# Layer one of a two-layer graph network: per-group statistics by one 128x512 product, sums and statistics added by two operations a tile

## The chip, the cores and the metric

One NeuronCore of one Trainium2 chip runs the whole program. The metric is the device time of one execution in microseconds. Engines are named as in the profile: PE is TensorE (PEld its weight loads), DVE is VectorE, ACT is ScalarE, POOL is GpSimd, SP is SyncE.

## What is computed

Two graph layers over 6,250 nodes of 128 channels and 106,250 edges sorted by destination. Only layer one is changed:

```python
h = jnp.maximum(_layernorm(x, axis=-1), 0.0)
x = nodes @ W + b_lin                      # nodes = h; 4 heads of 32 channels
sent, recvd = x[snd], x[rcv]
logits = leaky_relu(sum(concat(sent, recvd) * alpha, -1), 0.2)
e = jnp.exp(logits - segment_max(logits, rcv)[rcv])
att = e / segment_sum(e, rcv)[rcv]
out = segment_sum(att[:, :, None] * sent, rcv) + bias
```

The kernel needs, for every destination node, the weighted sum of its senders' rows (128 channels) and five statistics: two sums of weights, a count, and two maxima. A product with a 0/1 mask (edge x node) makes both from the edges of a tile.

## The kernel before

**Tiles, groups, rounds.** The edges are padded to 832 tiles of 128 edges. Four tiles (`TG`) are a group (208 groups), eight groups (`RG`) a round; the first and last round have four groups (`SPANS`). Below, k = 0 to 7 is a group's place in its round.

**POOL (L472).** One indirect DMA per tile gathers 128 rows of 130 numbers into a ring of 24 groups (`RING`). Before group g POOL waits until PE has finished group g - 24 (`agg0`).

**PE (L948 to L974).** For group g, `sum_stats` waits until DVE has added group g - 2 (`acc0`), then makes four products, one a tile: 5 columns of `edge_w` as weights, the tile's 128x128 mask moving, out to 5 lines of `stat_sums` at lines 32t, columns 128t. `sum_group` then makes four full products with the gathered rows as weights into `row_sums` and signals `agg0`. Sums and statistics of a group lie in two neighbouring banks of PSUM (`both_sums`), two such pairs in turn. At k = 0 `spread_delta` puts four one-column products (L937, L939) between the two.

**DVE (L663 to L691).** For group g it waits for `agg0`, then for each of the four tiles it makes the mask of a tile two groups on (L665) and adds sums and statistics of the tile in one operation of 128 lines by 2x128 numbers (L670) into `acc2`, at a column that a register gives. Each add first waits for the add before it (`acc0`), because their destinations overlap. Scaling of rows by their weights (L679) stands before a group, penalties (L603 to L615) after k = 0.

**Between rounds.** After k = 7, DVE scans the next round's logits for segment maxima (L625 to L651), with small PE transposes in between (L917 to L947). ACT makes the weights (L1138) and writes them into `edge_w` (L1144). Only then can k = 0 of the next round go through PE.

**End of layer one.** The last six groups' masks (`EARLY`) are made one round ahead. From L796 on, while the last two rounds run, finished blocks of nodes are transposed (L989, L995), divided and added to x. No gathers run from about 1343 us to 1476 us.

Of the kernel before, what the change touches and what calls it, by code (L numbers as in the profile page):

```python
# [7 lines left out]
P = 128  # L8
# [6 lines left out]
SH = 2  # L15
NB = (N + P - 1) // P
NPAD = NB * P
UA = 3
# [4 lines left out]
TG = 4  # L23
GE = TG * P
# [3 lines left out]
TILES = GROUPS * TG  # L28
ROUNDS = GROUPS // RG
EPAD = TILES * P  # L30
RT = RG * TG
# [3 lines left out]
LCOL = 5  # L35
RW = CH + SH
FW = CH + HEADS
Q4 = P // TG
# [8 lines left out]
WORK = UNITS_A + RAW // UA  # L47
# [5 lines left out]
RG1 = 12  # L53
WORK1 = UNITS + RAW1
PROJ_SLOTS = 3
LINE_SLOTS = 3
ACT_BATCH = 16
ACT_TURNS = 2
ACT_ROUND = P // ACT_TURNS
# [15 lines left out]
EARLY = range(GROUPS - 6, GROUPS)  # L75
# [11 lines left out]
def gnn_layers(nc, a, out, table1, table2, table3):  # L87
# [3 lines left out]
    ds = bass.ds  # L91

    ctx = ExitStack()
    with ctx:
# [3 lines left out]
        def sb(name, shape, dt=fp32, st=ctx):  # L98
            return st.enter_context(nc.sbuf_tensor(name, shape, dt))
# [23 lines left out]
        def sem(name):  # L123
            return ctx.enter_context(nc.semaphore(name))
# [4 lines left out]
        both_sums = [pair[n][:, :, :] for n in range(2)]  # L129
        row_sums = [bank[0], bank[2]]  # L130
        stat_sums = [bank[1], bank[3]]
# [5 lines left out]
        acc2 = sb("acc2", [P, 2, ACCW])  # L137
        acc = acc2[:, 0, :]
        acc_w = acc2[:, 1, :]
# [9 lines left out]
        onehot = sb("onehot", [P, 2, TG, P])  # L149
# [9 lines left out]
        with ExitStack() as st:  # L159
# [6 lines left out]
            own_scale, sum_scale = parts[:, 1], parts[:, 0]  # L166
            rows_x = sb("rows_x", [P, LINE_SLOTS, RW], st=st)
            offsets = sb("offsets", [FETCHED, P], i32, st)
            bias_all = sb("bias_all", [P, CH], st=st)
            dst_pair = sb("dst_pair", [P, 2 * TILES], i32, st)  # L170
            dst_int, first_all = dst_pair[:, 0:TILES], dst_pair[:, TILES:]
            IN_PAIR = 2 * TILES // P
            early_a = dst_pair[:, 0:IN_PAIR * P].bitcast(fp32).rearrange("p (t c) -> p t c", c=P)
            early_b = sb("early_b", [P, len(EARLY) * TG - IN_PAIR, P], st=st)
            dn = sb("dn", [SH * (RT + 2) - 2, 2, P + 2], i32, st)
# [18 lines left out]
            select_w = sb("select_w", [1, SH, P], st=st)  # L194
            factor = sb("factor", [P, 1], st=st)
            factor_w = sb("factor_w", [P, 1], st=st)
            edge_w = sb("edge_w", [P, 2, RT, LCOL], st=st)
            sizes = sorted({z for _, z in SPANS})
            pens = {z: sb(f"pens{z}", [1, 2, SH * (z * TG + 2)], st=st) for z in sizes}
            edge_of = {z: sb(f"edge_of{z}", [1, 2, SH * (z * TG + 2)], st=st) for z in sizes}  # L200
# [2 lines left out]

            normed = sb("normed", [P, 2, UA, CH], st=st)
            feats_t = sb("feats_t", [P, 2, UA * P], st=st)
            moments0 = sb("moments0", [P, WORK * UA, 6], st=st)
            mean_var0 = sb("mean_var0", [P, WORK * UA, 2], st=st)
            rows_w = moments0[:, :, :].rearrange("p m s -> p (m s)")[:, 0:2 * RW].rearrange("p (k c) -> p k c", k=2)
            std0 = sb("std0", [P, WORK * UA], st=st)
            rstd0 = sb("rstd0", [P, WORK * UA], st=st)  # L210
            shift0 = sb("shift0", [P, WORK * UA], st=st)
            w0 = sb("w0", [P, CH], st=st)
            w0_t = sb("w0_t", [P, CH], st=st)
            w0_ext = sb("w0_ext", [P, FW], st=st)
# [47 lines left out]
            def converted(r):  # L262
# [4 lines left out]
            bias_in, biased, dn_used, set_done, sc = (  # L267
                sem(n) for n in ("bias_in", "biased", "dn_used", "set_done", "sc"))
# [6 lines left out]
            oh0, scaled0, scaled_v, agg0, acc0 = (sem(n) for n in ("oh0", "scaled0", "scaled_v", "agg0", "acc0"))  # L275
            half_in = [sem(f"half_in{s}") for s in range(RING // HALF)]
            line_in = [sem(f"line_in{s}") for s in range(LINE_SLOTS)]
            lines_in, offsets_ready = sem("lines_in"), sem("offsets_ready")
# [73 lines left out]
            def line_total(j):  # L352

                return 16 * P * (j // LINE_SLOTS + 1)

            def row_of(n):

                if n in LINE_TILES:
                    return rows_x[:, LINE_TILES.index(n) % LINE_SLOTS, :]
                if n in ACT_TILES0:  # L360
# [9 lines left out]
            def mask_of(n):  # L370

                i = n - EARLY.start * TG
                if i < 0:
                    return onehot[:, n // TG % 2, n % TG, :]
                return early_a[:, i, :] if i < IN_PAIR else early_b[:, i - IN_PAIR, :]

            def scale_parts(g):

                n, end = g * TG, (g + 1) * TG
                cuts = sorted({n, end, *(x + d for x in LINE_TILES + ACT_TILES0 for d in (0, 1) if n <= x + d < end)})  # L380
                return list(zip(cuts, cuts[1:]))

            def scaled_until(g):

                return sum(len(scale_parts(v)) for v in range(g + 1))
# [18 lines left out]
            def first_sync(sp):  # L404
# [9 lines left out]
                def line(j):  # L414
                    if j >= LINE_SLOTS:
                        sp.wait_ge(agg0, LINE_TILES[j - LINE_SLOTS] // TG + 1)
                    for o in range(0, P, BATCH):
# [107 lines left out]
            def first_vector(dve):  # L525
# [1 line left out]
                dve.memset(stat_sums[1][:, :], 0.0).then_inc(set_done, 1)  # L527
                dve.memset(select[:, :, :], 0.0).then_inc(set_done, 1)
                dve.memset(select_w[:, :, :], 0.0).then_inc(set_done, 1)
                dve.memset(edge_w[:, :, :, SH:SH + 1], 1.0).then_inc(set_done, 1)  # L530
                for z in sizes:
                    dve.memset(pens[z][:, :, :], -BIG).then_inc(set_done, 1)
                    dve.memset(edge_of[z][:, :, :], -BIG).then_inc(set_done, 1)
                    dve.memset(lg_cols[z][:, :], 0.0).then_inc(set_done, 1)
                dve.wait_ge(set_done, 5 + 3 * len(sizes))
                for h in range(SH):
                    dve.memset(select[:, h, h * HC:(h + 1) * HC], 1.0).then_inc(set_done, 1)
                    dve.memset(select_w[:, h, h::Q4], 1.0).then_inc(set_done, 1)
# [46 lines left out]
                dve.wait_ge(dst_in, 16 * 2)  # L585
                dve.tensor_tensor(dst_rel[:, :], dst_int[:, :], first_all[:, :], ALU.subtract).then_inc(rel_done, 1)
                dve.wait_ge(bias_in, 16)
                dve.wait_ge(set_done, 5 + 2 * SH + 3 * len(sizes))
                dve.wait_ge(rel_done, 1)
                done = [0]  # L590

# [73 lines left out]
                    dve.tensor_scalar(mask_of(n), iota_row[:, :], dst_rel[:, n:n + 1], None, ALU.is_equal).then_inc(early_ready if n // TG in EARLY else oh0, 1)  # L665

                def add(n, v):
                    if n:
                        dve.wait_ge(acc0, n)
                    dve.tensor_tensor(acc2[:, :, ds(v, P)], acc2[:, :, ds(v, P)], both_sums[n // TG % 2][:, :, n % TG * P:(n % TG + 1) * P],  # L670
                                      ALU.add).then_inc(acc0, 1)

                def scale_rows(r, g):

# [150 lines left out]
                n = (g1 + 2) * TG  # L825
# [9 lines left out]
                n = (g1 + 3) * TG  # L835
# [25 lines left out]
            def first_tensor(pe):  # L861
# [40 lines left out]
                    last.then_inc(own_t, 1)  # L902
                for w in range(UNITS_A):
                    turn_own(w)
                pe.wait_ge(set_done, 5 + 2 * SH + 3 * len(sizes))

                def turn_penalties(r):
                    n, step = lines(r), SH * pitch(r)
# [40 lines left out]
                def sum_stats(r, g):  # L949
                    k = g - SPANS[r][0]  # L950
                    if k == 0:
                        pe.wait_ge(ew_ready, 2 * (r + 1))
                    if g in EARLY:
                        pe.wait_ge(early_ready, (g + 1 - EARLY.start) * TG)
                    else:
                        pe.wait_ge(oh0, (g + 1) * TG)
                    if g >= 2:
                        pe.wait_ge(acc0, (g - 1) * TG)
                    for t in range(TG):
                        pe.matmul(stat_sums[g % 2][t * Q4:t * Q4 + LCOL, t * P:(t + 1) * P], edge_w[:, r % 2, k * TG + t, :], mask_of(g * TG + t),  # L960
                                  start=True, stop=True)
                    if k == 0:
                        spread_delta(r)

# [81 lines left out]
            def first_scalar(act):  # L1046
# [52 lines left out]
                    act.copy(acc[SH * HC:, starts(w) * P:starts(w) * P + m], row_sums[w % 2][SH * HC:, 0:m]).then_inc(own_in, 1)  # L1099
                for w in range(UNITS_A):  # L1100
                    keep_own(w)
                act.wait_ge(set_done, 5 + 2 * SH + 3 * len(sizes))

                def keep_logits(r):
                    if r < RAW_TURNS:
# [619 lines left out]
```

## Time and profile before

| | us |
|---|---|
| median of 3 runs | 2840.2 (2838.53 to 2845.22) |
| profiled execution, its own time | 2840.72 |
| its span, first to last instruction | 2838.9 |
| PE / DVE / ACT / POOL busy | 1705.1 / 1536.6 / 588.7 / 1601.2 |
| L472, gathers of layer one, x782 | 742.7 busy, 950 ns each |
| L973, group sums, x1616 records | 382.3 busy, 411 ns each |
| L960, statistics, x1616 records | 116.3 busy, 377 ns each |
| L670, add of sums and statistics, x832 | 349.5 busy, 420 ns each |
| L665, masks in the loop, x808 | 235.6 busy, 292 ns each |

A timeline row gives start, busy time, engine, line, operation, out<-in, how many instructions were merged (x), and in brackets the idle time of the engine before it with what ended it. An fp32 product shows as two records, so x8 stands for four tiles. "remote" means that the profile did not find who released the wait. PEclk is the granted TensorE clock as a share of 2.4 GHz.

### The profile page before, as it was taken

The page shows a single profiled execution, that of the slowest core. Times are in us where ns is not written, and L with a number is a line of the kernel's source. Part 1 is how long each engine was busy: PE and PEld are TensorE (multiplying, and loading weights), DVE is VectorE, ACT ScalarE, POOL GpSimd, SP SyncE. Part 2 cuts the span into 40 slices and gives each one's busy share as a digit, 9 for nine tenths or more (in the row PEclk, how much of TensorE's full clock was granted, in tenths as well). Part 3 has the DMA queues.
Part 4 walks back from the last instruction along what each step waited for, and adds up shares of the span by engine and source line. Part 5 has one row for each costly group of instructions (what it writes and reads, how often), then busy time and mean ns, then how long its engine had stood idle before and what let it go on. Part 6 is the DMA issues. An engine that isn't in the chain of part 4 may idle for free.

```text
span 2838.9 us, 30406 instructions
## 1 busy us (share of the span) xinstructions
PE 1705.1 (60%) x8785; PEld 1185.5 (42%) x8785; DVE 1536.6 (54%) x5409; ACT 588.7 (21%) x1218; POOL 1601.2 (56%) x1703
## 2 busy tenths in 40 slices
PE   1444545444444444444644877787787787777778
PEld 1333334233333333333434544554454554454556
DVE  1455556554555545556754555555555555555557
ACT  1530000000000000000235333333333233333333
POOL 6425666665566665656063566666666665566650
PEclk6765555555555555555667888887888778888889
DMA  4201221221122111211042333333333333344332
GB/s 122 71 21 40 46 45 44 46 45 43 39 46 46 43 44 42 46 42 45 1 114 71 105 106 95 106 109 110 109 110 111 111 96 100 107 110 112 109 105 79
DMA packets 102330, 212.33 MB, mean 75 GB/s; under 512 B 30944, under 2 KB 65238, under 8 KB 92183
## 3 DMA queue, kind: packets, MB, share of 16 engines
q0 software_dynamic: 53120, 109.70, 15.7%
q1 hardware_dynamic: 46411, 99.73, 12.3%
q8 instruction: 72, 1.18, 0.2%
q10 hardware_dynamic: 2636, 0.98, 0.2%
q14 instruction: 91, 0.75, 0.1%
HBM read 197.40 MB, written 12.88 MB: 74 GB/s over the span
## 4 chain that ended last, share of the span: by engine, by line
PE 31%; DVE 23%; another core or an unknown queue 21%; issue 19%; ACT 4%; DVEq 1%; POOL 0%; DMA 0%; ACTq 0%; SPq 0%; POOLq 0%
DVE acc L670 9%; PE pair L1424 6%; PE bank L1433 6%; PE bank L1444 5%; PE pair L1418 4%; PE pair L973 4%; DVE onehot L665 2%; DVE acc L1627 2%; DVE onehot L1586 2%; DVE pre L1612 1%; PE pair L960 1%; DVE ef L1593 1%; PE bank L937 1%; ACT hidden L1503 1%
## 5 line engine op out<-in xcount | busy, mean ns | idle before, releaser
L1367 POOL DMA_INDIRECT acc<-table,index x830 | 786.1, 947 | 533.6 <-DVE pre L1612 268.5
L472 POOL DMA_INDIRECT rows<-table,index x782 | 742.7, 950 | 539.8 <-issue 214.5
L1627 DVE TENSOR_TENSOR acc<-acc,bank 128x128 f32 x832 | 239.5, 288 | 411.6 <-remote 188.0
L665 DVE TENSOR_SCALAR onehot<-iota_row,dst_rel 128x128 f32<-128x128 f32 x808 | 235.6, 292 | 408.3 <-remote 326.3
L1424 PE MATMUL pair<-hidden,we 128*128 128x512 f32 x416 | 281.6, 764 | 210.6 <-ACT hidden L1503 152.3
L973 PE MATMUL pair<-onehot,rows 128*128 128x128 f32 x1616 | 382.3, 411 | 0.0
L973 PEld LDWEIGHTS pair<-onehot,rows 128*128 128x128 f32 x1616 | 328.0, 301 | 68.6 <-issue 61.1
L1433 PEld LDWEIGHTS bank<-wn1b,ef 128*128 128x128 f32 x1664 | 273.3, 237 | 193.4 <-issue 100.6
L670 DVE TENSOR_TENSOR acc<-acc,pair 128x256 f32 x832 | 349.5, 420 | 5.4 <-PE pair L973 1.8
L1433 PE MATMUL bank<-wn1b,ef 128*128 128x128 f32 x1664 | 280.6, 324 | 52.4 <-DVE ef L1593 44.1
L1444 PE MATMUL bank<-onehot,msg 128*128 128x128 f32 x1664 | 261.9, 309 | 13.4 <-ACT msg L1516 8.8
L960 PE MATMUL pair<-onehot,edge_w 128*5 128x128 f32 x1616 | 116.3, 377 | 247.2 <-DVE acc L670 214.9
L1444 PEld LDWEIGHTS bank<-onehot,msg 128*128 128x128 f32 x1664 | 243.2, 225 | 18.9 <-ACT msg L1516 14.2
L1418 PE MATMUL pair<-ea,we 64*128 64x512 f32 x416 | 248.2, 678 | 0.0
L1503 ACT ACTIVATE hidden<-pair,be 128x512 f32<-128x512 f32 x208 | 141.2, 679 | 431.8 <-remote 293.5
L1424 PEld LDWEIGHTS pair<-hidden,we 128*128 128x128 f32 x416 | 71.2, 215 | 382.1 <-issue 192.6
L1516 ACT ACTIVATE msg<-pre 128x512 f32<-128x512 f32 x208 | 131.0, 630 | 426.7 <-DVE pre L1612 356.9
L1138 ACT ACTIVATE weights<-shifted 66x128 f32<-66x128 f32 (+1 forms) x27 | 8.3, 309 | 994.2 <-DVE shifted L650 835.5
L1593 DVE SCALAR_TENSOR_TENSOR ef<-pair,be,gate 128x512 f32<-128x512 f32 x208 | 155.4, 747 | 95.2 <-remote 51.0
L923 PE MATMUL bank<-ident,seg_max 66*1 66x66 f32 (+1 forms) x54 | 10.0, 287 | 308.9 <-issue 193.8
L1586 DVE TENSOR_SCALAR onehot<-iota_row,dst_rel 128x128 f32<-128x128 f32 x832 | 186.5, 291 | 0.1
L1612 DVE TENSOR_TENSOR pre<-bank,acc 128x512 f32<-128x512 f32 x208 | 142.4, 685 | 62.8 <-remote 37.9
(170 smaller groups left out, 1466.6 us busy)
## 6 DMA issues: line engine op xcount, KB each, us to landing
ts<-in_ts SPq DMA_DIRECT2D x52, 1024.0 KB
ea<-in_ea_t SPq DMA_DIRECT2D x52, 512.0 KB
acc<-table,index POOLq DMA_INDIRECT x830
rows<-table,index POOLq DMA_INDIRECT x782
table<-feat SPq DMA_DIRECT2D x16, 195.0 KB
table<-proj SPq DMA_DIRECT2D x12, 256.0 KB, 2.3
table<-x_rows SPq DMA_DIRECT2D x11, 256.0 KB, 2.3
out<-x_rows SPq DMA_DIRECT2D x11, 256.0 KB
```

Source lines behind the costliest of these rows:

```text
L472: gp.indirect_dma_start(rows0[:, n % (RING * TG), :], None, table1, bass.IndirectOffsetOnAxis(index[:, n:n + 1], 0)).then_inc(half_in[g % ...
L665: dve.tensor_scalar(mask_of(n), iota_row[:, :], dst_rel[:, n:n + 1], None, ALU.is_equal).then_inc(early_ready if n // TG in EARLY else oh0, 1)
L670: dve.tensor_tensor(acc2[:, :, ds(v, P)], acc2[:, :, ds(v, P)], both_sums[n // TG % 2][:, :, n % TG * P:(n % TG + 1) * P], ALU.add).then_i ...
L973: last = pe.matmul(row_sums[g % 2][:, t * P:(t + 1) * P], row_of(g * TG + t)[:, 0:CH], mask_of(g * TG + t), start=True, stop=True)
L1367: gp.indirect_dma_start(rows[:, g % RG1, t, :], None, table, bass.IndirectOffsetOnAxis(index[:, n:n + 1], 0)).then_inc(gathered[g % RG1], 16)
L1418: pe.matmul(bank[g % 2][:, :], we1[:, :], ea[:, g // HALF % 2, edges(g)], start=True, stop=True).then_inc(h1, 1)
L1424: pe.matmul(bank[2 + g % 2][:, :], we2[:, :], hidden[:, g % 2], start=True, stop=True).then_inc(h2, 1)
L1433: last = pe.matmul(bank[4 + g % 2][:, t * P:(t + 1) * P], ef[:, g % 2, t * P:(t + 1) * P], wn1b[:, :], start=True, stop=True)
L1444: last = pe.matmul(bank[6 + g % 2][:, t * P:(t + 1) * P], msg[:, g % 2, t, :], onehot[:, g % 2, t, :], start=True, stop=True)
L1586: dve.tensor_scalar(onehot[:, g % 2, t, :], iota_row[:, :], dst_rel[:, q:q + 1], None, ALU.is_equal).then_inc(oh1, 1)
L1593: dve.scalar_tensor_tensor(ef[:, g % 2], bank[2 + g % 2][:, :], be2[:, 0:1], gate[:, g % 2], ALU.add, ALU.mult).then_inc(efd, 1)
L1627: dve.tensor_tensor(acc[:, ds(v, P)], acc[:, ds(v, P)], bank[6 + g % 2][:, t * P:(t + 1) * P], ALU.add).then_inc(acc1, 1)
```

## The change

Each group's four statistics products become one: 32 columns (`Q4`) of `edge_w` per tile, five used and the rest zero, 4x32 = 128 weight columns, against the four masks side by side (128x512), a full bank of `stat_sums`. Tile t's statistics are the block of lines 32t and columns 128t, as before; the twelve mixed blocks are not read. The add becomes two operations: 32 lines by 128 of the statistics into `acc_w` with no wait of its own, then 128 by 128 of the sums into `acc` behind the `acc0` wait. `edge_w` grows and is cleared once at the start. To make room and to let a group's masks lie side by side, `early_a`/`early_b` are cut at whole groups, the opening layer norm's small buffers share the place of `early_b`, and an unused buffer shrinks.

```diff
-LINE_SLOTS = 3
+LINE_SLOTS = 1
...
-            IN_PAIR = 2 * TILES // P
+            IN_PAIR = 2 * TILES // GE * TG
...
-            edge_w = sb("edge_w", [P, 2, RT, LCOL], st=st)
+            edge_w = sb("edge_w", [P, 2, RT, Q4], st=st)
...
+            opening = early_b[:, :, :].rearrange("p t c -> p (t c)")
+            NS = WORK * UA
+            moments0 = opening[:, 0:6 * NS].rearrange("p (m s) -> p m s", s=6)
+            mean_var0 = opening[:, 6 * NS:8 * NS].rearrange("p (m s) -> p m s", s=2)
...
+            def masks_at(g):
+
+                i = (g - EARLY.start) * TG
+                if i < 0:
+                    return onehot[:, g % 2, :, :]
+                return early_a[:, i:i + TG, :] if i < IN_PAIR else early_b[:, i - IN_PAIR:i - IN_PAIR + TG, :]
...
-                dve.memset(edge_w[:, :, :, SH:SH + 1], 1.0).then_inc(set_done, 1)
+                dve.memset(edge_w[:, :, :, :], 0.0).then_inc(set_done, 1)
...
+                dve.memset(edge_w[:, :, :, SH:SH + 1], 1.0).then_inc(set_done, 1)
...
                 def add(n, v):
+                    b, t = n // TG % 2, n % TG
+                    own_lines, own_cols = slice(t * Q4, (t + 1) * Q4), slice(t * P, (t + 1) * P)
+                    dve.tensor_tensor(acc_w[own_lines, ds(v, P)], acc_w[own_lines, ds(v, P)], stat_sums[b][own_lines, own_cols], ALU.add)
                     if n:
                         dve.wait_ge(acc0, n)
-                    dve.tensor_tensor(acc2[:, :, ds(v, P)], acc2[:, :, ds(v, P)], both_sums[n // TG % 2][:, :, n % TG * P:(n % TG + 1) * P],
-                                      ALU.add).then_inc(acc0, 1)
+                    dve.tensor_tensor(acc[:, ds(v, P)], acc[:, ds(v, P)], row_sums[b][:, own_cols], ALU.add).then_inc(acc0, 1)
...
-                    for t in range(TG):
-                        pe.matmul(stat_sums[g % 2][t * Q4:t * Q4 + LCOL, t * P:(t + 1) * P], edge_w[:, r % 2, k * TG + t, :], mask_of(g * TG + t),
-                                  start=True, stop=True)
+                    pe.matmul(stat_sums[g % 2], edge_w[:, r % 2, k * TG:(k + 1) * TG, :].rearrange("p t c -> p (t c)"),
+                              masks_at(g).rearrange("p t c -> p (t c)"), start=True, stop=True)
```

## Rows read from the trace of the kernel before

**Rows 1.** Windows: us, busy (count) of PE, PEld, DVE, ACT, POOL, PEclk, DMA, GB/s

```profile
197.00:1343.00 1146.00, 530.48 (x3409) 392.56 (x3407) 622.45 (x2300) 30.07 (x151) 695.54 (x732) 0.56 0.20 44
1343.00:1476.00 133.00, 77.27 (x534) 58.80 (x535) 100.84 (x347) 36.85 (x142) 37.27 (x46) 0.65 0.17 46
```

**Rows 2.** Timeline of ACT: the weights of a round, once a round

```profile
225.75 0.31 ACT L1138 ACTIVATE weights<-shifted 66x128 f32<-66x128 f32 x1 [20.30 <-DVE shifted L650]
...
669.67 0.31 ACT L1138 ACTIVATE weights<-shifted 66x128 f32<-66x128 f32 x1 [43.10 <-DVE shifted L650]
...
721.91 0.31 ACT L1138 ACTIVATE weights<-shifted 66x128 f32<-66x128 f32 x1 [43.26 <-DVE shifted L650]
...
1319.70 0.31 ACT L1138 ACTIVATE weights<-shifted 66x128 f32<-66x128 f32 x1 [39.64 <-DVE shifted L650]
```

**Rows 3.** Timeline of POOL: the gathers that follow a wait

```profile
526.22 0.94 POOL L472 DMA_INDIRECT rows<-table,index  x1 [4.29 <-PE pair L973]
...
543.53 0.94 POOL L472 DMA_INDIRECT rows<-table,index  x1 [2.46 <-remote]
...
560.85 0.94 POOL L472 DMA_INDIRECT rows<-table,index  x1 [2.61 <-remote]
...
574.94 0.94 POOL L472 DMA_INDIRECT rows<-table,index  x1 [4.29 <-PE pair L973]
...
761.03 0.94 POOL L472 DMA_INDIRECT rows<-table,index  x1 [1.18 <-remote]
```

**Rows 4.** Timeline of DVE: after k = 0, k = 3, k = 6, and at the scan

```profile
204.27 0.28 DVE L779 TENSOR_TENSOR x_rows<-x_rows,bias_all 128x128 f32<-128x128 f32 x1
204.47 0.22 DVE L603 CAST line<-dn 66x130 f32<-66x130 int32 x1
...
543.29 0.29 DVE L665 TENSOR_SCALAR onehot<-iota_row,dst_rel 128x128 f32<-128x128 f32 x1 [4.35 <-remote]
...
560.61 0.29 DVE L665 TENSOR_SCALAR onehot<-iota_row,dst_rel 128x128 f32<-128x128 f32 x1 [9.08 <-remote]
560.81 0.42 DVE L670 TENSOR_TENSOR acc<-acc,pair 128x256 f32 x1
...
561.14 0.28 DVE L665 TENSOR_SCALAR onehot<-iota_row,dst_rel 128x128 f32<-128x128 f32 x1
...
565.02 0.41 DVE L625 TENSOR_TENSOR_SCAN fore<-pen_f,bank 66x128 f32<-66x128 f32 x1
```

**Rows 5.** Timeline of PE: k = 3, k = 6, then k = 0 of the next round

```profile
533.85 2.08 PE L973 MATMUL pair<-onehot,rows 128*128 128x128 f32 x8
...
548.81 1.62 PE L973 MATMUL pair<-onehot,rows 128*128 128x128 f32 x8
...
570.26 0.61 PE L960 MATMUL pair<-onehot,edge_w 128*5 128x128 f32 x8 [0.48 <-ACT edge_w L1144]
570.80 1.01 PE L937 MATMUL bank<-delta,select 1*128 1x1 f32 x4
...
572.59 2.08 PE L973 MATMUL pair<-onehot,rows 128*128 128x128 f32 x8
```

**Rows 6.** Waits of DVE from 197 to 1343 us: total, times, longest

```profile
DVE onehot L665 <- remote: 326.3, 58, 9.1
```

**Rows 7.** Timeline of PE in layer two: a full product of 128x512

```profile
2004.31 1.12 PE L1418 MATMUL pair<-ea,we 64*128 64x512 f32 x2
...
2014.55 2.08 PE L1424 MATMUL pair<-hidden,we 128*128 128x512 f32 x2 [5.23 <-ACT hidden L1503]
```

**Rows 8.** Windows around k = 0: columns as in rows 1

```profile
570.00:575.00 5.00, 4.74 (x32) 3.79 (x32) 1.91 (x7) 0.44 (x4) 0.71 (x2) 0.50 0.13 28
```

**Rows 9.** Timeline of the stretch without gathers: PE, then DVE without masks

```profile
1348.34 0.61 PE L960 MATMUL pair<-onehot,edge_w 128*5 128x128 f32 x8 [0.50 <-DVE acc L670]
...
1416.33 2.06 DVE L670 TENSOR_TENSOR acc<-acc,pair 128x256 f32 x4
...
1417.01 1.16 PE L973 MATMUL pair<-dst_pair,rows 128*128 128x128 f32 x8
```

More of the change, by code:

```diff
@@ L205, in gnn_layers @@
             feats_t = sb("feats_t", [P, 2, UA * P], st=st)
[L206 to L211, printed above, removed]
+            opening = early_b[:, :, :].rearrange("p t c -> p (t c)")
+            NS = WORK * UA
+            moments0 = opening[:, 0:6 * NS].rearrange("p (m s) -> p m s", s=6)
+            mean_var0 = opening[:, 6 * NS:8 * NS].rearrange("p (m s) -> p m s", s=2)
+            rows_w = opening[:, 0:2 * RW].rearrange("p (k c) -> p k c", k=2)
+            std0, rstd0, shift0 = (opening[:, (8 + i) * NS:(9 + i) * NS] for i in range(3))
             w0 = sb("w0", [P, CH], st=st)
@@ L587, in first_vector @@
                 dve.wait_ge(bias_in, 16)
-                dve.wait_ge(set_done, 5 + 2 * SH + 3 * len(sizes))
+                dve.wait_ge(set_done, 6 + 2 * SH + 3 * len(sizes))
                 dve.wait_ge(rel_done, 1)
@@ L904, in first_tensor @@
                     turn_own(w)
-                pe.wait_ge(set_done, 5 + 2 * SH + 3 * len(sizes))
+                pe.wait_ge(set_done, 6 + 2 * SH + 3 * len(sizes))
                 def turn_penalties(r):
@@ L1101, in first_scalar @@
                     keep_own(w)
-                act.wait_ge(set_done, 5 + 2 * SH + 3 * len(sizes))
+                act.wait_ge(set_done, 6 + 2 * SH + 3 * len(sizes))
                 def keep_logits(r):
```

## Prediction

> **What bounds the kernel now.** I read the windows by stage first. From 197 to 1343 us, layer one's rounds with gathers, no engine is full: of 1146 us PE is busy 530, DVE 622, POOL 696 [rows 1]. So a chain through several engines sets the time. The timeline of ACT shows its beat: L1138 runs once a round, 22 rounds lie between 225.75 and 1319.70, 49.7 us each; single rounds take 48.7 or, as from 669.67 to 721.91, 52.2 [rows 2]. Then I followed one round on POOL, DVE and PE side by side. POOL stands exactly one ring ahead: after 526.22, 543.53, 560.85 and 574.94 it runs on only when a wait has ended [rows 3]. DVE resumes 0.24 us before POOL at 543.29 and 560.61 [rows 4], so both wait for the same signal, `agg0` of k = 3 and of k = 6. The odd thing is that PE had long done both: k = 3 ended at 533.85 + 2.08 = 535.93 and k = 6 at 548.81 + 1.62 = 550.43 [rows 5]. The signals are seen 7.4 and 10.2 us later, both times about 2.5 us after POOL has run out of gathers it may issue [rows 3]. These late signals are DVE's "remote" waits, 326 us in all [rows 6]. Who holds them the profile does not say; it says that they come when POOL stops. Where no gathers run they are absent: there PE waits 0.50 us for DVE's add of two groups before [rows 9].
>
> So a round has three pieces, counted between POOL's restarts: 526.22 to 543.53 (17.3 us) and 543.53 to 560.85 (17.3) are twelve gathers each plus waits, (17.32 - 2.61) / 12 = 1.23 us a gather [rows 3]; 560.85 to 574.94 (14.1) is serial work. In the serial piece DVE adds k = 6 and k = 7 (560.61 to 565.02, eight tiles, 0.55 each) [rows 4], scans, PE turns and ACT makes weights until 570.26, then PE makes the statistics of k = 0 in 0.54 us, the one-column products in 1.79, the sums in 2.08, and POOL restarts [rows 5, 3]. Only this piece is bound by PE's and DVE's own speed.
>
> **Statistics by one product.** Removed: four 5-column products, eight records, from 570.26 to 570.80, 0.54 us [rows 5]. Their records last about 0.38 us each and still eight fit into 0.61, so they overlap. Added: one product of 128x512. Its price is in layer two: 2.08 us at half clock, 1.12 at full clock [rows 7]. At k = 0 the granted clock is 0.50 [rows 8]; PE has then done little for over ten microseconds. I take 2.08: +1.54 us at k = 0 of every round, on the path. At full clock it would be 1.12 against 0.40, about +0.7: that is the lower end. For k = 1 to 7 the same +1.54 lies beside waits: PE's chain for k = 3 grows by at most 4 x 1.54 = 6.2 us less what already waits for DVE, and k = 3's signal has 7.4 us to spare; k = 6's chain, counted from k = 3's signal, passes k = 4 to 6, grows by at most 4.6 and has 10.2. So nothing shows as long as the lateness keeps its date. If that cover is gone, it costs 1.54 a product. What is late next is POOL's wait for k = 2: its run of eight gathers after 526.22 would stop a microsecond or two, inside the piece that ends at 543.53.
>
> Eight records of four products show 0.61 us where a single full-width product of the same 512 columns shows 2.08 [rows 5, 7]. The Trainium skill, page "TensorEngine Tiling (Array Packing)", section "Overview", gives up to four times the speed for a side of at most 32, which this change gives up; rows and rule agree. The same page, section "Key Properties", says that a change of tiling mode drains TensorE. That rule speaks for the change, which removes two mode changes a group. By the rule there would be a gain outside the four products; the rows leave it no more than a share of the 0.54, since 570.80 follows 570.26 by just that.
>
> **Two operations for one add.** Before: mask and add together take 0.55 us a tile; the add of 256 columns lasts 0.42, then the next add waits for it and starts about 0.14 later, and the mask hides in between [rows 4]. After: mask, statistics add, sums add. The trace has no 32x128 add. Slots nearest to it are start to start: mask to next 0.20 (560.61 to 560.81), a 128x128 add to next 0.20 (204.27 to 204.47) [rows 4]. Three slots give 0.60; one more register instruction a tile may show, so I take 0.63, +0.08 a tile. Lower end: 0, if slots pack a little closer; upper end: three full busy times of 0.28, 0.84, +0.29. The wait for the sums add before no longer shows, since two operations lie behind it. On the path are the eight tiles of k = 6 and 7: 8 x 0.08 = +0.6 us a round (0 to 2.3). The adds of k = 0 to 5, +0.3 a group, lie under the same late signals as the products. Where no masks are made (last groups), four adds take 2.06 us [rows 9]; two short operations with an add chain of 0.28 + 0.14 give about 1.7, -0.3 a group.
>
> **Costed at nothing.** Clearing `edge_w` (2048 numbers a line) at the start, a few microseconds at most on DVE: the opening waits for x and the biases, and waits later hide it. The shared buffers, the wider stride of `edge_w` for ACT's writes: same sizes of operations. No DMA or POOL instruction is added or moved.
>
> **The sum.** Rounds with gathers: 22 x (1.54 + 0.64) = 22 x 2.18 = 48.0 us. Outside of them: k = 0 of the first short round +1.5; the round after 1319.70, of which only part has gathers, +3.5; the 16 full groups from 1361 to 1419 without gathers: PE has 0.50 us of slack a group [rows 9], so each costs between 0.3 (DVE sets the pace) and 1.0 (PE does), 0.6 taken, 9.6, and their two k = 0 +3.1; the last four groups +3.0; eight groups without masks -2.4. Together +18.3. Layer two is untouched. 48.0 + 18.3 = +66.3 on the profiled execution's 2840.7 gives 2907.0; that execution lies 0.5 above the median of 2840.2, so I forecast 2907 (rounded). A measurement of this kernel tells 0.3%, 8.5 us, from no change.
>
> **The rivals.** *(a) The lateness is a delay after PE's end, not a date set by POOL.* Then what makes k = 3 and k = 6 end later passes through. At half clock k = 3 ends some 2.9 us later (k = 1 to 3 back to back in PE at 4.1 us each against 9.95 us now) and k = 6 some 3.3: +6.2 a round on top, 22 x 6.2 = 136, 3043 us. At full clock products shrink by as much as the new one adds, and little is left; halfway is 2975. For it: the same lateness of the second signal in most rounds. Against it: each signal falls about 2.5 us behind POOL's stop [rows 3]. Chance 0.2.
>
> *(b) The extra serial time is taken back by shorter stops.* The waits of POOL that end "remote" are 2.61 us at 560.85 but 1.18 at 761.03 [rows 3]. If products that end later make them 1.2 instead of 2.5, two a round give back 2.6 of the 2.2: about 2845 with the tail. Chance 0.12.
>
> *(c) Faster: the clock.* PE does more in the same time; if that keeps the granted clock at 1.0 up to k = 0, the serial piece has 1.12 for the product, 1.79 / 2 = 0.9 for the one-column products and 1.16 for the sums [rows 7, 9], 3.2 instead of 4.4, with DVE's +0.6 a gain of 0.6 a round: 22 x 0.6 = 13 us, tail about even, 2828. It decides from the point where the clock at k = 0 is over 0.75. Against it: PE idles through the scan whatever the product takes, and rows 8 show 0.50. Chance 0.08; other gains 0.02.
>
> *(d) Other beat.* Rounds of 48.7 and of 52.2 us exist [rows 2], six of the 22 are long. All long would be 16 x 3.5 = +56 on my sum, 2963; none long -21, 2886. This widens my case, it isn't one of its own.
>
> **How the numbers follow.** My case, with 2870 to 2965 as its own range, has 0.5; (a) 0.2; (b) 0.12; (c) and other gains 0.1; what I have not thought of on the slow side 0.08. Predicted is the likeliest, 2907. The range for 8 in 10 leaves out (c) and the upper part of (a): 2846 to 2990. Faster by over 0.3%: 0.10; within: 0.12; slower: 0.78.
>
> **What would show it.** In the profile of the changed kernel: L960 as two records, about 2.08 us together, with the one-column products 2.1 instead of 0.54 us behind its start; the way from DVE's start on k = 6 to POOL's restart 16.3 us instead of 14.1; tiles at 0.63 us; POOL's pieces of twelve gathers still near 17.3; L1138 about 51.9 us apart. A piece of twelve gathers of 19 us or more means (a); a beat still under 50 means (b); a PEclk of 1.0 at k = 0 means (c). I would be wrong above all if the unknown holder of PE's signals depends on PE's instructions themselves, since the change takes six product records and six weight loads a group out of PE's stream.

## The result and the profile after

The changed kernel takes 2944.8 us (median of 4 runs, 2941.4 to 2951.7), the kernel before 2842.7 beside it: ratio 1.036, 95% interval 1.034 to 1.039. It is slower by 102 us; forecast was 2907, +66. The kernel before itself took 2837 to 2867 us in some of the later comparisons and 2168 to 2176 us in others (one slow execution of 2523 us left out), one and the same chip among both, so that every kernel is set against the runs of before made beside it, and those of the first kind are called "beside 2843", those of the second "beside 2172".

The timeline of ACT of the changed kernel, the line that makes a round's weights (L1147, before L1138) [rows 2], shows where the time went:

```profile
228.18 0.31 ACT L1147 ACTIVATE weights<-shifted 66x128 f32<-66x128 f32 x1 [19.95 <-DVE shifted L658]
282.65 0.31 ACT L1147 ACTIVATE weights<-shifted 66x128 f32<-66x128 f32 x1 [42.77 <-DVE shifted L658]
...
609.54 0.31 ACT L1147 ACTIVATE weights<-shifted 66x128 f32<-66x128 f32 x1 [43.08 <-DVE shifted L658]
661.51 0.31 ACT L1147 ACTIVATE weights<-shifted 66x128 f32<-66x128 f32 x1 [40.60 <-issue]
...
1402.66 0.31 ACT L1147 ACTIVATE weights<-shifted 66x128 f32<-66x128 f32 x1 [43.17 <-DVE shifted L658]
...
1520.22 0.31 ACT L1147 ACTIVATE weights<-shifted 34x128 f32<-34x128 f32 x1 [12.74 <-DVE shifted L658]
```

The same 22 rounds take 1174.5 us (228.18 to 1402.66) instead of 1093.9: +80.5. Up to the first of them +2.4. From the last to the last weights of all 117.6 us instead of 99.7 (1319.70 to 1419.37): +17.9. From there to the end of the span 1419.4 instead of 1419.5: layer two pays nothing. Together +100.7, the difference of the two spans, 2939.6 and 2838.9. There are again two kinds of rounds: 52.0 us (609.54 to 661.51; nine of them, 51.9 on average) and 54.4 (228.18 to 282.65; thirteen), where before had sixteen of 48.8 and six of 52.2 on average [rows 2].

The timeline of POOL, those gathers that follow a stop, says what sets the two kinds. A run is here the gathers between two stops, and a piece is a run with the stop that ends it:

```profile
562.65 0.94 POOL L479 DMA_INDIRECT rows<-table,index  x1 [9.55 <-PE pair L982]
...
579.90 0.94 POOL L479 DMA_INDIRECT rows<-table,index  x1 [2.30 <-PE pair L982]
...
602.75 0.94 POOL L479 DMA_INDIRECT rows<-table,index  x1 [3.10 <-remote]
...
617.00 0.94 POOL L479 DMA_INDIRECT rows<-table,index  x1 [9.55 <-PE pair L982]
...
634.23 0.94 POOL L479 DMA_INDIRECT rows<-table,index  x1 [2.33 <-PE pair L982]
...
651.50 0.94 POOL L479 DMA_INDIRECT rows<-table,index  x1 [2.60 <-remote]
...
668.97 0.94 POOL L479 DMA_INDIRECT rows<-table,index  x1 [7.79 <-PE pair L982]
```

From 617.00 to 668.97 POOL runs twelve gathers, twelve and eight, each followed by a stop: 17.23, 17.27 and 17.47 us. Before, the same three pieces took 17.31, 17.32 and 14.09 [rows 3]. The first two are as they were; all of +3.38 lies in the serial piece. From 562.65 to 617.00 the runs are twelve, sixteen and four, and the piece that ends with k = 0 takes 14.25 though it holds four gathers only: k = 6 was added before it, k = 7 in it (DVE starts on them at 594.73 and 602.52). Other long rounds have twelve, twelve, four and four, like the long ones of before.

The serial piece itself, on DVE (k = 6 from 651.27, its scan at 657.59) and on PE:

```profile
651.27 0.29 DVE L673 TENSOR_SCALAR onehot<-iota_row,dst_rel 128x128 f32<-128x128 f32 x1 [6.68 <-remote]
651.47 0.27 DVE L678 TENSOR_TENSOR acc<-acc,pair 32x128 f32 x1
651.66 0.27 DVE L681 TENSOR_TENSOR acc<-acc,pair 128x128 f32 x1
651.86 0.27 DVE L673 TENSOR_SCALAR onehot<-iota_row,dst_rel 128x128 f32<-128x128 f32 x1
652.16 0.28 DVE L678 TENSOR_TENSOR acc<-acc,pair 32x128 f32 x1
652.46 0.29 DVE L681 TENSOR_TENSOR acc<-acc,pair 128x128 f32 x1
...
657.59 0.41 DVE L633 TENSOR_TENSOR_SCAN fore<-pen_f,bank 66x128 f32<-66x128 f32 x1
```

```profile
662.82 2.08 PE L969 MATMUL pair<-onehot,edge_w 128*128 128x512 f32 x2 [0.47 <-ACT edge_w L1153]
664.83 1.01 PE L947 MATMUL bank<-delta,select 1*128 1x1 f32 x4
665.71 0.99 PE L949 MATMUL bank<-delta,select_w 1*128 1x1 f32 x4
666.62 2.08 PE L982 MATMUL pair<-onehot,rows 128*128 128x128 f32 x8
```

The eight tiles take 6.32 us (651.27 to 657.59), before 4.41 (560.61 to 565.02) [rows 4]: +1.91, 0.24 a tile. The product takes 2.01 us until the next begins (662.82 to 664.83), before 0.54 [rows 5]: +1.47. The two make the whole 3.38. The slots show where the tile loses: its first three operations start 0.20 us apart, but in the second tile, whose statistics are on lines 32 to 63, L678 starts 0.30 after the mask and L681 0.30 after L678, each just behind the end of the operation in front (651.86 + 0.27, 652.16 + 0.28). Six of the eight tiles have two such slots. The third tile of each group has a longer mask as well (0.34 and 0.48 us, at 652.66 and 655.75), and the add behind it waits for that too; why this mask is longer no run tells.

The windows, and the waits of DVE, of the changed kernel (columns as in rows 1 and 6):

```profile
197.00:1343.00 1146.00, 563.43 (x2132) 379.91 (x2132) 709.54 (x2822) 27.36 (x138) 650.65 (x684) 0.70 0.19 41
662.80:668.70 5.90, 5.88 (x19) 4.36 (x20) 1.54 (x5) 0.23 (x2) 0.00 (x0) 0.50 0.00 0
```

```profile
DVE onehot L673 <- remote: 170.5, 41, 6.7
```

In the same stretch the mean granted clock is 0.70 instead of 0.56 [rows 1], yet around k = 0 it is still 0.50, the lower level, 1.2 GHz, and the product takes 2.08 us. DVE's wait for late signals is 170.5 us instead of 326.3 [rows 6]: DVE is busy for 87 us more in it, and the longer adds seem to fill part of the time in which it had waited.

### The profile page after: what moved, and what is told of

Same layout as the page of the kernel before. It is cut to its first block, busy times and chain, and to the rows that moved or that the text cites. A ratio compares the mean times of both kernels' runs of the same rounds, so it can differ in the third digit from the quotient of the medians.

```text
span 2939.6 us, 29540 instructions
## 1 busy us (share of the span) xinstructions
PE 1804.9 (61%) x7537; PEld 1211.5 (41%) x7537; DVE 1693.0 (58%) x6242; ACT 588.4 (20%) x1218; POOL 1603.3 (55%) x1703
## 4 chain that ended last, share of the span: by engine, by line
PE 29%; DVE 28%; issue 21%; another core or an unknown queue 16%; ACT 4%; DVEq 2%; POOL 0%; ACTq 0%; POOLq 0%
DVE acc L681 7%; DVE acc L678 6%; PE pair L1433 6%; PE bank L1442 5%; PE bank L1453 5%; PE pair L1427 4%; PE pair L982 3%; PE pair L969 3%; DVE acc L1636 3%; DVE onehot L673 3%; DVE onehot L1595 2%; DVE pre L1621 1%; DVE ef L1602 1%; PE bank L947 1%
## 5 line engine op out<-in xcount | busy, mean ns | idle before, releaser
L969 PE MATMUL pair<-onehot,edge_w 128*128 128x512 f32 x404 | 316.5, 876 | 258.6 <-DVE acc L681 163.9
L673 DVE TENSOR_SCALAR onehot<-iota_row,dst_rel 128x128 f32<-128x128 f32 x808 | 237.0, 294 | 256.8 <-remote 173.7
L982 PEld LDWEIGHTS pair<-onehot,rows 128*128 128x128 f32 x1616 | 295.5, 259 | 128.4 <-issue 117.7
L982 PE MATMUL pair<-onehot,rows 128*128 128x128 f32 x1616 | 297.0, 345 | 0.0
L678 DVE TENSOR_TENSOR acc<-acc,pair 32x128 f32 x832 | 235.1, 283 | 40.6 <-issue 20.8
L1427 PE MATMUL pair<-ea,we 64*128 64x512 f32 x416 | 255.3, 696 | 0.0
L681 DVE TENSOR_TENSOR acc<-acc,pair 128x128 f32 x832 | 236.2, 284 | 30.8 <-issue 22.5
L1147 ACT ACTIVATE weights<-shifted 66x128 f32<-66x128 f32 (+1 forms) x27 | 8.4, 309 | 1035.2 <-DVE shifted L658 710.1
L969 PEld LDWEIGHTS pair<-onehot,edge_w 128*128 128x128 f32 x404 | 83.0, 255 | 283.7 <-DVE onehot L673 142.9
```

The lines of the kernel that those rows point to most:

```text
L678: dve.tensor_tensor(acc_w[own_lines, ds(v, P)], acc_w[own_lines, ds(v, P)], stat_sums[b][own_lines, own_cols], ALU.add)
L681: dve.tensor_tensor(acc[:, ds(v, P)], acc[:, ds(v, P)], row_sums[b][:, own_cols], ALU.add).then_inc(acc0, 1)
L969: pe.matmul(stat_sums[g % 2], edge_w[:, r % 2, k * TG:(k + 1) * TG, :].rearrange("p t c -> p (t c)"), masks_at(g).rearrange("p t c -> p (t ...
L982: last = pe.matmul(row_sums[g % 2][:, t * P:(t + 1) * P], row_of(g * TG + t)[:, 0:CH], mask_of(g * TG + t), start=True, stop=True)
L1427: pe.matmul(bank[g % 2][:, :], we1[:, :], ea[:, g // HALF % 2, edges(g)], start=True, stop=True).then_inc(h1, 1)
```

## The experiments

**Theories.** *Serial:* only what lies between DVE's start on k = 6 and the sums of k = 0 costs time, 1.47 for the product and 1.8 to 1.9 for the adds; the rest is hidden under the late signals. *Delay:* what the products add at k = 1 to 7 passes through as well. For the adds: *held* (an operation on other lines than the last waits for its end) against *third operation* (it costs as such).

**One half of the change at a time, beside 2843.** product_only keeps before's add (and has the change's buffers):

```
-for t in range(TG):
-    pe.matmul(stat_sums[g % 2][t * Q4:t * Q4 + LCOL, t * P:(t + 1) * P], edge_w[:, r % 2, k * TG + t, :], mask_of(g * TG + t), ...)
+pe.matmul(stat_sums[g % 2], edge_w[:, r % 2, k * TG:(k + 1) * TG, :]..., masks_at(g)..., start=True, stop=True)
 dve.tensor_tensor(acc2[:, :, ds(v, P)], acc2[:, :, ds(v, P)], both_sums[...], ALU.add).then_inc(acc0, 1)
```

> The kernel before with the change's single product of 128 by 512 a group, and the one add of 256 columns kept; what the product puts into the mixed blocks is added too, so the statistics are not the reference's. If the new product costs its own time at k = 0 alone (1.47 us in the trace of the change, L969 at 610.85 to L947 at 612.86 against 0.54): 22 x 1.47 = 32 us in the rounds, 1.5 in the first short round, some 3 in the round after the last full beat, some 10 to 14 in the stretch without gathers: +48 us, 2891, and ACT's weights 51.2 us apart on average. If what products delay at k = 1 to 7 passes through as well, each piece of twelve gathers grows from 17.3 to over 19 us and the time is 2940 or more. If the later product is taken back by shorter stops: under 2860.

adds_only keeps before's four products:

```
-dve.tensor_tensor(acc2[:, :, ds(v, P)], acc2[:, :, ds(v, P)], both_sums[...], ALU.add).then_inc(acc0, 1)
+dve.tensor_tensor(acc_w[own_lines, ds(v, P)], acc_w[own_lines, ds(v, P)], stat_sums[b][own_lines, own_cols], ALU.add)
+dve.tensor_tensor(acc[:, ds(v, P)], acc[:, ds(v, P)], row_sums[b][:, own_cols], ALU.add).then_inc(acc0, 1)
```

> The kernel before with the change's two adds a tile, and the four small products kept. If a tile of 0.775 us instead of 0.55 is on the path for the eight tiles of k = 6 and k = 7 alone: 22 x 1.8 = 40 us, and some 10 to 15 in the stretch without gathers: +53 us, 2896. The sum of this run's and product_only's difference should then be the whole change's +102 within 10 us. If the slower tile comes only together with the wide product (a wait for PE rather than DVE's own pace): no more than +20, 2863.

Measured: product_only 2899.2, ratio 1.020 (1.016 to 1.024); adds_only 2911.3, ratio 1.025 (1.021 to 1.029). The ratios add up to +4.5%, the change shows +3.6%. Both halves cost time, each 8 to 15 us more than expected, and their sum, +124 us, lies 22 above the change's +102 where 10 was the most expected: they are not additive. ACT's weights split the two profiled runs: product_only +48.7 in the 22 rounds and +2.2 in the stretch behind them; adds_only +51.4 and +12.9. POOL's stops in product_only show what its rounds are made of:

```profile
336.77 0.95 POOL L479 DMA_INDIRECT rows<-table,index  x1 [4.92 <-PE pair L980]
...
353.27 0.95 POOL L479 DMA_INDIRECT rows<-table,index  x1 [1.64 <-issue]
...
365.33 0.95 POOL L479 DMA_INDIRECT rows<-table,index  x1 [2.36 <-remote]
...
663.01 0.94 POOL L479 DMA_INDIRECT rows<-table,index  x1 [2.99 <-remote]
...
692.23 0.94 POOL L479 DMA_INDIRECT rows<-table,index  x1 [9.44 <-PE pair L980]
...
715.00 0.94 POOL L479 DMA_INDIRECT rows<-table,index  x1 [2.99 <-remote]
```

Some of its early rounds run twelve, eight and twelve gathers with stops of 1.6, 2.4 and 4.9 us, 48.2 to 48.4 us a round, less than before's short ones in spite of the product. From 530 us on all run sixteen and sixteen with stops of 3.0 and 7 to 11 us, 48 to 56 us. The 32 gathers take some 39.5 us in either; the round is these and its stops, and where the stops fall decides more than 1.47 us do. *Delay* in its full size falls: all rounds would have been some 6 us dearer, and the pieces of twelve outside the serial one are here 16.5 us (336.77 to 353.27), not over 19. But the 22 rounds cost 2.2 us each on average, not 1.47, and what brings the sixteens about, the products of k = 1 to 7 perhaps, no run tells. adds_only runs twelve, eight, twelve in nearly every round, with other stops:

```profile
568.17 0.94 POOL L472 DMA_INDIRECT rows<-table,index  x1 [2.60 <-remote]
...
590.87 0.94 POOL L472 DMA_INDIRECT rows<-table,index  x1 [8.03 <-PE pair L975]
...
602.51 0.94 POOL L472 DMA_INDIRECT rows<-table,index  x1 [1.75 <-PE pair L975]
...
619.81 0.94 POOL L472 DMA_INDIRECT rows<-table,index  x1 [2.61 <-remote]
```

22.70, 11.64 and 17.30, together 51.6.

The same kernel once more, on another chip, where before took 2851.7:

> The kernel before with the change's two adds a tile and its own four small products at every k, the same kernel as adds_only. Where before takes some 2172 us: k0_small differs from it only in the single products of k = 1 to 7. If these lie hidden beside DVE's adds: k0_small_b's 2209 within 4 us, ratio 1.017, the weights of a round 39.1 us apart. If they count: 7 x 1.5 = 10 us a round less, which POOL's 40 us of gathers then cut off, 2185 to 2195. Where before takes some 2840 us: 2911 again.

2972.4, ratio 1.044 (1.038 to 1.049): the same runs of gathers, but the long stop is 9.5 us in nearly all rounds, against 7.4 to 9.5 in adds_only's, and a round takes 53.6 instead of 52.1. So the adds alone cost between 2.5% and 4.4% from one chip to another; a run of it beside 2172, which would separate the adds from the products of k = 1 to 7, is missing.

**Why a tile is slow.** Two kernels, alike but for the lines; the two lines with own_lines are in q0_scratch alone, own_scratch keeps the change's. The statistics are left out of both outputs:

```
+scratch = feats_t[:, :, :].rearrange("p k c -> p (k c)")
-own_lines = slice(t * Q4, (t + 1) * Q4)
+own_lines = slice(0, Q4)
-dve.tensor_tensor(acc_w[own_lines, ds(v, P)], acc_w[own_lines, ds(v, P)], stat_sums[b][own_lines, own_cols], ALU.add)
+dve.tensor_tensor(scratch[own_lines, own_cols], acc_w[own_lines, ds(v, P)], stat_sums[b][own_lines, own_cols], ALU.add)
```

> The changed kernel, but the statistics add of every tile reads and writes lines 0 to 31, and its result goes to a spare place, so the statistics are left out of the output. Same number and sizes of operations as own_scratch. If the tile's 0.775 us come from operations that start on lines other than the last one's and are held until it has finished, all three slots are 0.20 and a tile is 0.60 to 0.63: 1.4 us less a round for eight tiles, 22 x 1.4 = 31 us, and up to 8 in the stretch without gathers: 30 to 39 us under own_scratch. If the cost is that of a third operation as such: no difference to own_scratch (within 3 us).

> The control of q0_scratch: the statistics add goes to the same spare place but on the lines that the change gives it (0, 32, 64, 96 for the four tiles); the statistics are left out of the output. Expected at the changed kernel's time, 2945, within 5 us, with tiles of 0.775 us, if the place of the result costs nothing; 5 to 10 less if the computed address of the output cost time.

Measured: 2939.7 and 2940.3, where *held* had forecast 30 to 39 us between them. By the times alone it would have fallen; the traces say otherwise. The second tile of a group in own_scratch has the held slots of the change:

```profile
600.62 0.27 DVE L673 TENSOR_SCALAR onehot<-iota_row,dst_rel 128x128 f32<-128x128 f32 x1
600.91 0.28 DVE L680 TENSOR_TENSOR feats_t<-acc,pair 32x128 f32<-32x128 f32 x1
601.21 0.29 DVE L683 TENSOR_TENSOR acc<-acc,pair 128x128 f32 x1
```

Its four tiles take 3.10 us until the scan (600.02 to 603.12); q0_scratch's take 2.37 (598.33 to 600.70), every operation 0.20 us behind the one in front: 0.18 less a tile with nothing changed but the lines. Here is q0_scratch_b, the same kernel run again later:

> The changed kernel with the statistics add of every tile on lines 0 to 31 and its result in a spare place, so the statistics are left out of the output; the same kernel as q0_scratch. Where before takes some 2172 us and DVE's pace sets the rounds (after_b: 40.3 to 41.6 us apart): if operations that start on other lines are held, a tile of 0.60 instead of 0.775 us makes 32 x 0.175 = 5.6 us a round less, POOL's 40.5 us of gathers bound the rounds as in before, and what stays is the product at k = 0 where POOL does not bind and the stretch without gathers: 2180 to 2195. If the third operation as such is what costs: 2245 as after_b. Where before takes some 2840 us: 2940 again.

It came beside 2851.7 and took 2957.5 (ratio 1.036, 1.031 to 1.042). Its DVE (first and second tile of k = 6, then the scan) and its POOL:

```profile
811.32 0.29 DVE L673 TENSOR_SCALAR onehot<-iota_row,dst_rel 128x128 f32<-128x128 f32 x1 [8.74 <-remote]
...
811.92 0.27 DVE L673 TENSOR_SCALAR onehot<-iota_row,dst_rel 128x128 f32<-128x128 f32 x1
812.11 0.27 DVE L680 TENSOR_TENSOR feats_t<-acc,pair 32x128 f32<-32x128 f32 x1
812.31 0.27 DVE L683 TENSOR_TENSOR acc<-acc,pair 128x128 f32 x1
...
816.06 0.40 DVE L633 TENSOR_TENSOR_SCAN fore<-pen_f,bank 66x128 f32<-66x128 f32 x1
```

```profile
811.55 0.95 POOL L479 DMA_INDIRECT rows<-table,index  x1 [2.61 <-remote]
...
827.43 0.94 POOL L479 DMA_INDIRECT rows<-table,index  x1 [6.00 <-PE pair L984]
```

All slots are 0.20 us, eight tiles take 4.74 us (811.32 to 816.06) instead of 6.32, and the serial piece with eight gathers 15.88 instead of 17.47: 1.58 and 1.59. Set against the change, the lines alone are worth 0.20 us a tile, of which the held slots make 0.15 and the longer mask of the third tile, absent here, most of the rest; the third operation is worth (4.74 - 4.41) / 8 = 0.04. That fits a rule of the Trainium skill, page "VectorE: DVE Perf Modes", section "Two Vector instructions with no wait between them": an instruction whose input or output starts in another group of 32 lines than the last input from, or output into, the same memory is held until every earlier Vector instruction has finished. The tile on line 32 shows it above, those on 64 and 96 do the same, the one on line 0 does not.

Where the gain went in the rounds is again a matter of runs: in q0_scratch no round has the runs of twelve, twelve and eight; they are made up of runs of twelve, sixteen and four, 53.9 us on average, against own_scratch's two kinds of 52.0 and 54.4, 53.5 on average. In q0_scratch_b four of 22 are of the twelve, twelve, eight kind, and they take 50.6 to 50.7 us. Where POOL gathers nothing, the gain is there at once; the weights of q0_scratch, then of own_scratch:

```profile
1413.15 0.31 ACT L1149 ACTIVATE weights<-shifted 66x128 f32<-66x128 f32 x1 [43.12 <-DVE shifted L658]
...
1518.74 0.31 ACT L1149 ACTIVATE weights<-shifted 34x128 f32<-34x128 f32 x1 [8.38 <-DVE shifted L658]
```

```profile
1405.02 0.31 ACT L1149 ACTIVATE weights<-shifted 66x128 f32<-66x128 f32 x1 [43.31 <-DVE shifted L658]
...
1523.03 0.31 ACT L1149 ACTIVATE weights<-shifted 34x128 f32<-34x128 f32 x1 [13.27 <-DVE shifted L658]
```

105.6 against 118.0 us: 12.4 less, nearly the 12.9 that the adds cost there in adds_only.

**The product at k = 0, beside 2172.** The changed kernel, with small products at k = 0:

```
+if k == 0:
+    for t in range(TG):
+        pe.matmul(stat_sums[g % 2][t * Q4:t * Q4 + LCOL, t * P:(t + 1) * P], edge_w[:, r % 2, k * TG + t, 0:LCOL], mask_of(g * TG + t), ...)
+else:
     pe.matmul(stat_sums[g % 2], edge_w[:, r % 2, k * TG:(k + 1) * TG, :]..., masks_at(g)..., start=True, stop=True)
```

> The changed kernel, but at k = 0 of each round the statistics come from four products of 5 columns, as before; at k = 1 to 7 from the single product. If only the product at k = 0 lies on the path and POOL's runs of gathers keep their lengths: 22 x 1.47 = 32 us in the rounds and some 4 outside, 2908. If what the products delay at k = 1 to 7 is what costs: an eighth of the product's share comes back, no more than 8 us, 2937. If POOL's runs fall into other lengths, as they did between own_scratch and q0_scratch (rounds of 12, 12 and 8 gathers there 52.0 us, of 12, 16 and 4 there 54.4), the gain in the rounds is between 0 and 32 us while the stretch without gathers gains its 3 in any case.

It took 2207.6, ratio 1.016 (1.014 to 1.018), where POOL does not stop as it does beside 2843, so its expectation, reckoned from those stops, was not put to the test. The changed kernel was not beside it, so both went together:

> The changed kernel with four products of 5 columns at k = 0 of each round and the single product at k = 1 to 7, as in k0_small, beside the changed kernel on one chip. On a chip where the kernel before takes some 2840 us: 1.47 us less in each of 22 rounds and in the two k = 0 of the end, 35 us under the changed kernel if POOL's runs keep their lengths, 5 to 35 if they change; no more than 8 if the products at k = 1 to 7 are what costs. On a chip like that of k0_small, where before takes some 2173 us and DVE was never held: 2208 again, +35 over before.

> The changed kernel, unaltered. On a chip where before takes some 2840 us: 2945 again, ratio 1.036. On a chip where before takes some 2173 us: there k0_small's rounds took 39.06 us at their own pace and POOL's gathers need 40 to 40.5; the single product at k = 0 adds 1.5 us, so rounds of 40.5 us, 23 x 1.5 = 34 us over k0_small, 2242, ratio 1.032. If the product at k = 0 were hidden there behind DVE's adds: 2208.

k0_small_b 2208.9, ratio 1.017 (1.015 to 1.019); after_b 2244.9, ratio 1.033 (1.032 to 1.035). The 36.0 us between them are 1.3 for each of the 27 rounds. The weights of k0_small_b, then of after_b:

```profile
246.97 0.31 ACT L1152 ACTIVATE weights<-shifted 66x128 f32<-66x128 f32 x1 [30.22 <-DVE shifted L658]
...
1103.21 0.31 ACT L1152 ACTIVATE weights<-shifted 34x128 f32<-34x128 f32 x1 [12.09 <-DVE shifted L658]
```

```profile
252.04 0.31 ACT L1147 ACTIVATE weights<-shifted 66x128 f32<-66x128 f32 x1 [30.23 <-DVE shifted L658]
...
1140.87 0.31 ACT L1147 ACTIVATE weights<-shifted 34x128 f32<-34x128 f32 x1 [12.10 <-DVE shifted L658]
```

The 22 rounds between take 856.2 and 888.8 us, 38.9 and 40.4 each: 1.48 us a round on average for the product at k = 0. Here no signal is late. Single rounds differ by 1.1 to 1.4 us in the first half and by 0.9 to 2.5 in the second, so that the average comes as near to the 1.47 of the traces as it does is in part chance; that the product at k = 0 costs most of its own time is not. The same test beside 2843 is missing. What is left of after_b's cost, 36.6 us, belongs to the adds and the products of k = 1 to 7 together; in k0_small DVE waits only 17.8 us in all for PE's sums and PE 174 us for DVE's adds, so I take it for the adds, but that is argued, not shown.

**Edits that might beat before, beside 2172.** All three ran there:

```
 spread_late:  -if k == 0: spread_delta(r)   (ahead of the sums)
               +if k == 0 and r == LAST: spread_delta(r)
               +if stats and g == SPANS[r][0]: spread_delta(r)   (behind them)
 coarse_wait:  -if g >= RING: gp.wait_ge(agg0, g - RING + 1)
               +if g >= RING and g % RG == 0: gp.wait_ge(agg0, min(g - RING + RG, GROUPS - RING))
 pair67:       +gp.wait_ge(agg0, g - RING + 1 + (g % RG == 6))
```

> The kernel before with the four one-column products of k = 0 and their copy moved behind the sums product, in all rounds but the last. POOL's gathers go on 1.8 us earlier after k = 0, and DVE's adds of k = 0 begin up to 0.9 us later. If POOL's runs and stops set the round: 22 x 1.8 = 39 us less, 2803. If the round hangs on DVE's adds of k = 0: 0 to 20 us more, up to 2862. If POOL's runs fall into the long pattern (52.2 instead of 48.7 us): the gain is eaten, 2840.

> The kernel before, but POOL waits for PE's signals once a round instead of once a group: the first gather of a round waits for the eight groups whose places its gathers take. If PE's signals reach POOL and DVE only when POOL stops or nearly stops, DVE adds nothing during the 40 us of gathers and the chain then runs behind them: a round of 55 us or more, 3000 us or more. If the late signals have nothing to do with POOL's issuing, POOL no longer stops within a round and rounds take 40 to 42 us: 2650 to 2700.

> The kernel before, but at k = 6 POOL waits for k = 7's signal too, so it goes on with eight gathers instead of four and four. If the long rounds (52.2 us, six of 22) are long because k = 6 and k = 7 have a stop each: they become rounds of 48.7 to 49.5, some 16 to 21 us less, 2820 to 2826. If k = 7's signal takes as long to come as its own stop takes now (2.2 us more in every round of that kind, nothing in the others): within 8 us of before.

2173.7 (ratio 1.000, 0.9995 to 1.001), 2184.6 (1.005, 1.003 to 1.006) and 2173.3 (1.002, 0.999 to 1.005). None is faster, and coarse_wait is slower by 0.5%. Their expectations were reckoned from POOL's stops beside 2843, which are absent here, and were not put to the test. A wait of ACT in pair67, which has before's time here, tells why nothing is gained:

```profile
ACT lg_cols L1124 <- DMA rows<-table,index: 595.6, 21, 32.2
```

ACT waits 596 us for gathered rows: from 357 us on POOL, which issues without a stop, sets the round at 40.5 us, so what is saved elsewhere is worth nothing. Beside 2843, where POOL stops and the three would tell something, they were not tried, so whether PE's signals wait for POOL's stop there stays open.

## Why the prediction came out as it did

The sign, the range (2846 to 2990) and the case (2870 to 2965) hold; 2907 was 38 us short. By its steps:

- *What bounds the kernel.* Right: a serial piece between POOL's restarts, and pieces of twelve gathers that stay at 17.3 [rows 3]. They measured 17.23 and 17.27. It holds for the kernel beside 2843 only: beside 2172 POOL never stops like that, and the prediction had no sign of such a case.
- *The product, +1.54 on the path at k = 0 and nothing at k = 1 to 7.* Right on the path of the changed kernel: +1.47 in its trace, with the one-column products at 1.79 us as before and the pieces of twelve no longer than before. Taking it away at k = 0 gave 1.3 to 1.5 a round (k0_small_b against after_b), though beside 2172. The granted clock of 0.50 at k = 0 held. Less sure is the nothing at k = 1 to 7: in product_only a round grew by 2.2, and how much of that the other products cause stays open.
- *The tile, +0.08.* Wrong, and the largest miss: 0.24 (6.32 against 4.41 for eight). I took slots of 0.20 from operations that all begin on line 0 [rows 4]; three of four statistics adds begin on line 32, 64 or 96, where the add and the one behind it are held, 0.30 a slot. For a statistics add on line 0 the estimate would have been 0.04 too high (0.59 against 0.63). On the path this term is 1.91 a round, not 0.64: 22 x 1.27 = 28 us against the 34 by which the profiled runs miss the sum. It is within the term's own upper end, 2.3, which counted every operation at its full busy time.
- *Kinds of rounds.* Named as rival (d), but put at nothing in the sum. The short rounds grew by 3.1 (48.8 to 51.9): 69 us. Thirteen instead of six are long, each by 2.4 over a short one instead of 3.4: 13 x 2.4 less 6 x 3.4 is another 11. Together 80, the +80.5 of ACT's weights, where the sum had 48.0. The 11 had no term; what makes a round long is not shown. The tile's 28 and these 11 are more than the 32.5 that the sum missed in the rounds, because the product was 0.07 a round cheaper and a short round grew by 3.1 where the serial piece shown grew by 3.4.
- *Outside the rounds, +18.3.* It measured 20.3 (2.4 + 17.9), but by two errors that cancel. I had about +21 there, most of it for the products, and -2.4 for the adds without masks; product_only shows +2.2 behind the last full round and adds_only +12.9. So the product hides there, mostly under PE's waits for DVE's adds, and adds without a mask are held as well: four tiles take 2.25 us (1512.78 to 1515.03) where before's four took 1.98 (1413.25 to 1415.23).
- *The rivals.* (a), a delay, 2975: refuted by product_only's short rounds and the pieces of 17.3. (b), shorter stops, 2845 (its own terms give 2850): in the rounds of twelve, twelve and eight the stops after the twelves are 2.3 to 2.6 us in both. (c), the clock: the mean rose to 0.70, but where the path runs it stayed at 0.50. By the terms of (c) the gain would begin at some 0.84, not 0.75: 3.2 / 0.84 + 0.6 is the 4.4 of before.

## What to carry to other kernels

Price a vector operation on part of the lines by a row in which the starting lines change from one operation to the next as they will in the new kernel. Where they do not change, neighbours started 0.20 us apart here; where they do, count an operation's full busy time, 0.30 us here, before the next one starts. A change that makes one wide product of four narrow ones must show that the narrow ones did not already run side by side: here four took 0.54 us where one wide takes 2.0 at the same granted clock of 0.50. And where a producer's stops set the beat, test both halves of a change alone: they need not add up.

## What the runs showed of the hardware

Beside 2172 the gathers last about as long as beside 2843 (0.97 us on average in pair67, 0.95 in before's trace), yet the late signals of PE are gone: DVE in pair67 has no wait put down as remote at all, where before had 326 us of them [rows 6], though POOL gathers on without a stop, and layer two, counted from the last weights, is shorter too, 1100 us instead of 1419. So the lateness is not made by POOL's gathers alone, as the prediction's wording suggests, and what makes it stays open. Coarse_wait shows that signals arrive while POOL runs 32 gathers on end, when they are not late. The change itself costs nearly the same share in both, 3.6% and 3.3%, though the chain that sets the rounds is another.
